# A graph network on one core: edge product of the mean pass in float32r parts, node phases in a new order, registers read earlier

## The reference, cut to what matters

```python
h = relu(layernorm(x))                                # layer norm, no weights
# L0, the mean layer: the message is made from the DESTINATION's features
msg    = relu(concat(h[dst], edge_attr_16) @ W1 + b1)
aggr   = segment_sum(msg, dst) / max(count(dst), 1)
x      = x + relu(aggr + h @ Wres + bres)
# L1: layer norm again, then three transformer convolutions (2, 2 and 1 heads)
h      = relu(layernorm(x))
for l in 0, 1, 2:
    e     = edge_attr_32 @ We
    alpha = sum(q[dst] * (k[src] + e)) / sqrt(C)      # softmax over the edges of a node
    h     = segment_sum(softmax(alpha) * (v[src] + e), dst) + h @ Ws + bs
x      = x + h                                        # PReLU between the layers
```

## Time and profile before

| what | us |
|---|---|
| median of three runs | 6319.2 |
| the profiled execution: its own time | 6324.56 |
| its span in the trace | 6322.9 |
| setup and `first` (to the mean pass's first edge product) | 0 to 71 |
| mean pass | 71 to 529 |
| `mean_end` | 529 to 611 |
| three attention passes with their node phases | 611 to 6323 |

### The profile page before, as it was taken

How to read it: one execution, slowest core, us unless ns; L and a number is a source line. 1 busy time by engine, 2 the same in 40 slices (tenths; PEclk the granted TensorE clock), 3 DMA queues, 4 the chain that set the end, 5 groups by cost and what they waited for, 6 DMA issues and landing times. The chain is left out here.

```text
span 6322.9 us, 195109 instructions
## 1 busy us (share of the span) xinstructions
PE 5496.1 (87%) x49308; PEld 4056.9 (64%) x49308; DVE 5504.6 (87%) x18553; ACT 2823.5 (45%) x12163; POOL 4385.8 (69%) x4735
## 2 busy tenths in 40 slices
PE   7996888888888887889888888888888888888887
PEld 5775666666666666666666666666666666666665
DVE  6556999999999998999999898988899899898988
ACT  3223555555555555455555555555333333333333
POOL 1223777777777775777777777775777777777775
PEclk9998999999999998999999999998899999999998
DMA  4554343333333333333333333333433333333333
GB/s 126 159 159 112 101 103 100 102 101 102 100 103 101 101 101 102 102 102 102 101 101 101 101 103 101 101 101 99 105 103 101 101 101 101 104 101 101 101 101 83
DMA packets 732940, 662.52 MB, mean 105 GB/s; under 512 B 421004, under 2 KB 558158, under 8 KB 732878
## 3 DMA queue, kind: packets, MB, share of 16 engines
q0 software_dynamic: 148544, 293.76, 18.8%
q1 hardware_dynamic: 555242, 315.06, 18.3%
q10 hardware_dynamic: 29092, 52.97, 2.7%
HBM read 639.39 MB, written 21.78 MB: 105 GB/s over the span
## 5 line engine op out<-in xcount | busy, mean ns | idle before, releaser
L1935 POOL DMA_INDIRECT Gall<-KV,sdn x4440 | 4234.5, 954 | 1377.6 <-issue 1272.7
L1220 ACT ACTIVATE vals<-vj,vals 128x32 f32<-128x32 f32 (+1 forms) x7960 | 1796.6, 313 | 19.3
L1154 PE MATMUL pG<-KVH,ohB 128*128 128x512 f32 (+1 forms) x2574 | 1176.4, 460 | 221.7 <-DVE cont L887 184.5
L1213 ACT ACTIVATE vals<-dd 128x16 f32<-128x16 f32 (+1 forms) x606 | 131.8, 217 | 2705.1 <-DVE dd L1022 2668.2
L1154 PE MATMUL pG<-KVH,ohA 128*128 128x512 f32 (+1 forms) x2574 | 1116.3, 434 | 11.8 <-DVE fw L975 0.6
L1154 PE MATMUL pG<-KVL,ohB 128*128 128x512 f32 (+1 forms) x2574 | 1072.2, 417 | 0.0
L1154 PE MATMUL pG<-KVL,ohA 128*128 128x512 f32 (+1 forms) x2574 | 1000.9, 392 | 0.0
L1147 PE MATMUL pY<-O,vals 128*66 128x42 f32 (+1 forms) x10576 | 778.9, 237 | 0.0
L1154 PEld LDWEIGHTS pG<-KVH,ohB 128*128 128x128 f32 x2574 | 530.0, 206 | 381.8 <-issue 260.9
L1147 PEld LDWEIGHTS pY<-O,vals 128*66 128x66 f32 (+1 forms) x10576 | 705.9, 143 | 46.9 <-ACT vals L1227 34.1
L1154 PEld LDWEIGHTS pG<-KVH,ohA 128*128 128x128 f32 x2574 | 494.7, 192 | 149.2 <-issue 8.6
(11 more groups left out here) (265 smaller groups left out, 8477.0 us busy)
## 6 DMA issues: line engine op xcount, KB each, us to landing
db<-D SPq DMA_DIRECT2D x606, 256.0 KB, 3.9
ea<-in_ea SPq DMA_DIRECT2D x606, 128.0 KB
Gall<-KV,sdn POOLq DMA_INDIRECT x4440
db<-D ACTq DMA_DIRECT2D x202, 256.0 KB, 3.5
qw<-QT SPq DMA_DIRECT2D x1818, 5.2 KB
dr<-in_dr SPq DMA_DIRECT2D x1212, 4.0 KB
ea<-in_ea SPq DMA_DIRECT2D x202, 64.0 KB, 3.5
sdn<-in_sdn SPq DMA_DIRECT2D x606, 12.0 KB
```

The lines of the kernel that those rows point to most:

```text
L1154: p = e.matmul(pG[:, 0:128 * m], table[:, n, :], half[:, 4 * q:4 * q + m, :].rearrange("p t c -> p (t c)"), start=n == 0 and h == 0, stop= ...
L1213: return e.activation(vals[u][:, :, 64:64 + H], dd[:, :, 0:H], ACT.Exp, scale=scale)
L1220: i = e.activation(vals[u][:, j, C * h:C * h + C], vj[u][:, j, C * h:C * h + C], ACT.Identity, scale=vals[u][:, j, 64 + h:65 + h])
L1935: e.indirect_dma_start(G[u][:, j, :], None, kvtab, bass.IndirectOffsetOnAxis(ap=sdn[u][:, j:j + 1], axis=0)).then_inc(s_g[u], 16)
```

## The change

- **Edge product.** `ea` is loaded as 64 rows: four tiles x 16 attributes, the two halves of the block side by side in the columns. ScalarE (`a_hi`) copies it as float32r into rows 0 to 63 of a new buffer `eap`, VectorE (`v_lo`) puts what is left into rows 64 to 127. The weights `bdp` are the float32r copy of W1's block diagonal (four tiles, rows 0 to 63 and again 64 to 127), and the rest of it. The product is four float32r matmuls of 256 columns. In each step ScalarE has one more operation (ahead of `relu`), VectorE one more (behind `OT`); the edge product waits for `v_lo`, and SyncE's load of `ea` waits for the `v_lo` of three blocks earlier.
- **Node phases.** Parts are now 4, 4, 3 and 2 chunks. The squares go to ScalarE (`square_A`). The norm is cut into `center`, `spread` and `scale_rows`, and folds (in `mean_end`) or the query work (in `first`) stand between them; TensorE's and ScalarE's programs take the chunks one after another with a lead of two. The norm of part 0 and the centring of part 1 of `first` (`vector_early`) stand in the middle of `vector_setup`.
- **Weights.** SyncE loads those of `first` with a semaphore of their own, which alone `first` waits for, then those of layer 0; GpSimd issues those of layers 1 and 2.
- **Registers.** In the last iteration of an attention pass the places are read ahead of the steps, also those of the drain.

```diff
+    bdp = sb("bdp", [128, 2, 256], F32R)
+    eap = nc.alloc_sbuf_tensor_at("eap", [128, 3, 256], F32R, offset=nc.sbuf_base - 256 * T)
...
-                "V": ["C acc", "Z src", "Z O", "Z OT"],
+                "V": ["C acc", "Z src", "Z O", "Z OT", "Z lo"],
                 "P": ["A e", "B agg7", "A q"],
-                "A": ["A relu"],
+                "A": ["Z hi", "A relu"],
...
+        def a_hi(e, s):
+            u = s.slot
+            ge16(e, s_e, 1, s)
+            after(e, "P", "e", s - 3)
+            return e.activation(eap[0:64, u, :], ea[u][0:64, :], ACT.Copy)
+
+        def v_lo(e, s):
+            u = s.slot
+            after(e, "A", "hi", s)
+            return e.tensor_tensor(eap[64:128, u, :], ea[u][0:64, :], eap[0:64, u, :].bitcast(F32), ALU.subtract)
...
-            return e.matmul(pE[u][:, :], ea[u][:, 0:128], bd16[:, :], start=True, stop=False)
+            after(e, "V", "lo", s)
+            hold(e)
+            for h in range(2):
+                for k in range(2):
+                    p = e.matmul(pE[u][:, 256 * h:256 * h + 256], eap[:, u, 128 * h:128 * h + 128], bdp[:, k, :],
+                                 start=h == 0 and k == 0, stop=False)
+            return p
...
             if not att and not fresh(s):
-                after(e, "P", "e", s - 3)
+                after(e, "V", "lo", s - 3)
                 hold(e)
...
+                e.dma_start(ea[u][0:64, :].rearrange("p (h c) -> p h c", h=2),
+                            eat[bass.ds(b, 1)].rearrange("a (h p) c -> p (a h) c", h=2)).then_inc(s_e[u], 16)
...
+        def vector_mean_end(e):
+            for c in chunks_of[0]:
+                fold_V_ops(e, c)
+            for n in range(NP):
+                nx = chunks_of[n + 1]
+                center(e, n)
+                for c in nx[:1]:
+                    fold_V_ops(e, c)
+                spread(e, n)
+                for c in nx[1:2]:
+                    fold_V_ops(e, c)
+                scale_rows(e, n)
+                for c in nx[2:]:
+                    fold_V_ops(e, c)
+
+        def vector_early(e):
+            e.wait_ge(s_x, 16)
+            center(e, 0)
+            center(e, 1)
+            spread(e, 0)
+            scale_rows(e, 0)
+
+        def vector_first(e):
+            for n in range(1, NP):
+                was = chunks_of[n - 1]
+                if n > 1:
+                    center(e, n)
+                    query_V(e, was[0])
+                spread(e, n)
+                query_V(e, was[1 if n > 1 else 0])
+                scale_rows(e, n)
+                for c in was[2 if n > 1 else 1:]:
+                    query_V(e, c)
+            for c in chunks_of[NP - 1]:
+                query_V(e, c)
...
+        def scalar_mean_end(e):
+            square_A(e, 0)
+            root_A(e, 0)
+            for n in range(NP):
+                cs = chunks_of[n]
+                soon = n == NP - 2
+                columns_A(e, cs[0])
+                if soon:
+                    square_A(e, n + 1)
+                for c in cs[1:2]:
+                    columns_A(e, c)
+                for k, c in enumerate(cs):
+                    rows_A(e, c)
+                    if k == 0 and soon:
+                        root_A(e, n + 1)
+                    if k == 1 and not soon and n + 1 < NP:
+                        square_A(e, n + 1)
+                    for x in cs[k + 2:k + 3]:
+                        columns_A(e, x)
+                if n + 1 < NP and not soon:
+                    root_A(e, n + 1)
...
         def vector_drain(e, n):
-            for s in (s3, s2, s1, s0):
-                base_of[s.c] = base_at(e, s)
...
-            if "D" in on:
+            if "D" in on and not last:
                 base_of[dt.c] = base_at(e, dt)
...
+                ends = [At(n, c + z.peel) for c in (-1, 0, 1, 2)]
                 for c in range(1 + z.peel, 4 + z.peel):
+                    base_of[c - 2] = base_at(e, At(whole, c - 2))
+                    for s in {2: ends[0:2], 3: ends[2:4]}.get(c - z.peel, []):
+                        drained[s.c] = base_at(e, s)
                     vector_step(e, At(whole, c), FULL, last=True)
+                base_of.update(drained)
```

More of the change, by code:

```diff
@@ L260, in sync_setup, with layer_weights @@
         e.dma_start(pra[:, :], a["prelu"].rearrange("(a m) -> a m", a=1).to_broadcast([128, 1])).then_inc(s_w, 16)
+    def layer_weights(e, l, landed):
+        for m, c in enumerate("kvqs"):
+            e.dma_start(wn[0:64, l + 1, 64 * m:64 * m + 64], a[f"W{c}{l}"]).then_inc(landed, 16)
+            e.dma_start(wn[64:65, l + 1, 64 * m:64 * m + 64], row(a[f"b{c}{l}"], 1)).then_inc(landed, 16)
+        for j in range(4):
+            e.dma_start(bd32[32 * j:32 * j + 32, l, 64 * j:64 * j + 64], a[f"We{l}"]).then_inc(landed, 16)
     def scalar_setup(e):
@@ L437, in build @@
     tiles_of = [min(4, NT - 4 * c) for c in range(NG)]
-    PART = 4
-    parts = [(c, min(c + PART, NG)) for c in range(0, NG, PART)]
+    parts = [(0, 0)]
+    while NG - parts[-1][1] > 5:
+        parts.append((parts[-1][1], parts[-1][1] + 4))
+    left = NG - parts[-1][1]
+    parts += [(NG - left, NG - left // 2), (NG - left // 2, NG)]
+    parts = [p for p in parts if p[1] > p[0]]
+    NP = len(parts)
+    part_of = [next(n for n, p in enumerate(parts) if p[0] <= c < p[1]) for c in range(NG)]
     s_kv = [sem(f"kv_landed{k}") for k in range(SL)]
@@ L460, in node_phase @@
         if norm:
-            rounds = [(range(*parts[n]) if n < len(parts) else (), range(*parts[n - 1]) if n else (),
-                       range(*parts[n - 1]) if n else ()) for n in range(len(parts) + 1)]
+            rounds = []
         elif tables:
@@ L468, in node_phase @@
         late = range(NG) if kv is not None else ()
+        chunks_of = [list(range(*p)) for p in parts] + [[], []]
         fold_V = ["den", "rcp", "avg", "val"] + {"mid": ["neg", "act"]}.get(kind, ["xr"])
         end_V = fold_V[-1]
-        norm_V = ["sum", "mean", "cen", "sq", "ssq", "var", "rstd", "nrm"]
+        center_V, spread_V, scale_V = ["sum", "mean", "cen"], ["ssq", "var"], ["rstd", "nrm"]
         col_bank = (pE[2], pY)
@@ L529, in tensor @@
                 for c in ta:
-                    if kv is not None:
-                        rows_P(e, c)
-                    else:
-                        query_P(e, c)
+                    rows_P(e, c)
+            if kind == "mean":
+                tensor_mean(e)
+            if kind == "first":
+                tensor_first(e)
             if between is not None:
@@ L586, in scalar @@
             for n, (fo, co, ta) in enumerate(rounds):
-                if norm:
-                    for c in co:
-                        columns_A(e, c)
-                    if fo:
-                        ts = slice(4 * fo[0], min(4 * fo[-1] + 4, NT))
-                        e.wait_ge(own["V"], pV["var", n])
-                        e.activation(st[:, 2, ts], st[:, 1, ts], ACT.Sqrt).then_inc(own["A"], 1)
-                if tables and not norm:
+                if tables:
                     for c in co:
@@ L597, in scalar @@
                 for c in ta:
-                    if kv is not None:
-                        rows_A(e, c)
-                    else:
-                        query_A(e, c)
+                    rows_A(e, c)
+            if kind == "mean":
+                scalar_mean_end(e)
+            if kind == "first":
+                scalar_first(e)
             for c in late:
@@ L687, in vector @@
                         fold_V_ops(e, c)
-                if norm and fo:
-                    norm_V_ops(e, n, fo)
-                if kv is None:
-                    for c in ta:
-                        query_V(e, c)
+            if kind == "mean":
+                vector_mean_end(e)
+            if kind == "first":
+                vector_first(e)
             if between is not None:
```

229 lines of the change are left out of this document (171 added, 58 removed).

## The result

The changed kernel takes 6370.9 us (median of four runs, 6361.4 to 6375.8) against 6319.4 (6319.1 to 6323.5) for the kernel before, measured on the same chip: ratio 1.0079, 95% interval 1.0067 to 1.0091. It is slower by some 51 us; 6300 was forecast. Its profiled execution took 6367.76 us, 43.2 more than that of before (6324.56). Two executions further down, one of the kernel before (14927 us) and one of `old_product` (12862), took twice as long as all others of the same kernel; the ratios leave them out, and without it the median of `old_product` would be 6307.6 instead of 6308.9.

The account below looks back on a forecast made before the run. SyncE's queue was taken to bound the mean pass at 2.24 us a block, VectorE the other stages. Edge product +2, `first` -7, `mean_end` -9, attention ends -5 sum to -19 us: median 6300.2 us, range 6288 to 6314.

Parts of the forecast that it names:

- the part on the edge product: Mean pass: shorter product hidden behind SyncE's queue, new ea load issued in 0.36 us like now; +2 us, between 0 and +8.
- TensorE's floor: Mean pass: a step's matmuls with the old product take TensorE 2.10 us, less than SyncE's 2.24.
- the second floor: Mean pass without SyncE: sums to node part, to relu, to next sums take 2.10 us, without the edge product.
- Rival 3: Mean pass: the three-dimensional load needs an extra shape instruction on SyncE, 0.129 us a block, +26 us, 6326; chance 0.07.
- Rival 1: Node phases: square not in the root's table set, 12 more loads on ScalarE, about 10 us in the path, 6310; chance 0.07.
- Rival 2: Node phases stay bound, by TensorE at half clock: -3 and -5 instead of -7 and -9, 6308; chance 0.13.
- Rival 4: Mean pass: chain of hi, lo and product longer than thought, SyncE waits; 0.1 us a block, +20 us, 6320; chance 0.04.
- Rival 6: Mean pass: TensorE's clock falls to its lower level in a tenth of the blocks, +22 us, 6322; chance 0.03.
- Both have room: Mean pass: with the added operations VectorE needs 2.03 us at most and ScalarE 1.4, within the 2.24 us step.
- Rival 5: Mean pass: SyncE is not the bound, so the pass falls to 2.10 us a block, 28 us less, 6270; chance 0.04.
- Node phases: Less VectorE work and waiting: first -7 us (-11 to -3), mean_end -9 us (-12 to -5).
- Early reads: Attention passes' ends: register reads moved to where the step begins win 5 us, between -7 and -2.

Follow-up runs that it names:

- old_product: Experiment 2: the changed kernel with the float32 edge product and plain load of before, keeping its node phases, weights and early reads; 6308.9 us, ratio 0.998.
- flat_load: The changed kernel with edge features laid out by the host as 64 plain rows of 256 numbers, so the ea load is plain; 6343.4 us.
- before_3d_load_128: The kernel before with the three-dimensional ea load from the fourth block on, its float32 product still reading 128 rows; 6373.6 us, ratio 1.0084.
- experiment 10: old_product with the ea loads issued by GpSimd instead of SyncE; 6285.9 us, ratio 0.9944.
- before_3d_load: The kernel before with the three-dimensional ea load and its float32 product reading 64 of the 128 rows; 6741.9 us.
- experiment 9: flat_load with ea loads issued by GpSimd and the edge product's first two matmuls done twice; mean pass at 2.328 us a step.

## Why the prediction was wrong

**The step that failed** is in the part on the edge product: "The new `ea` pattern has three dimensions. The nearest issue of that kind, the store of KV, takes 0.36 us, like now." It takes 0.63 us, with a register or without. The row was the wrong neighbour: the KV store has 128 rows, the new load 64, and 64 plain rows already cost 0.49 (`flat_load`); the second piece in each of them adds the other 0.14. The term was priced +2 (0 to +8); it measured +54 by itself (`before_3d_load_128`).

**The bound was right, which is why the error was dear.** That SyncE's queue sets the pass at 2.24 us and TensorE's floor is 2.10 held: 2.238 in experiment 2, and 2.10 in most stretches of experiment 10 (2.18 to 2.19 in the others, where GpSimd stood). So did the second floor, which has no edge product in it, nearly: 2.05 to 2.09 for the 2.10 worked out, and it is why a shorter product could win almost nothing even with SyncE out of the way. Whoever has shown that a queue is full has shown that each ns added to it counts 199 times; the forecast then took its one new instruction from a row on which nothing depended, and the upper bound of +8 left no room for a longer issue (0.04 us a block).

**Rival 3 had the mechanism**, a dearer three-dimensional issue with SyncE as the bound, and the point from which it decides (0.095 us a block). Its price of 0.129 us, an extra shape instruction, was wrong in kind: no such instruction came, the issue itself grew, by 0.27. It got a chance of 0.07, and the range was drawn to rivals 1 and 2 and ended at 6314, below even rival 3's own 6326.

**Rivals 4 and 6 hid behind it.** With the load cheap, the chain holds the pass at 2.2 instead of 2.10, and GpSimd's stands with the clock dips behind them add some 0.05. "Both have room" was true of each engine's sum of work and said nothing of the ring: the 1.4 us given from `ea` at X to the product took no account of the `db` issue, which stands between relu and the upper part in ScalarE's program. Rival 6's sign was right too: in the changed kernel waits at the product of 0.2 to 0.7 us, in a step that also has 0.4 us less work, went with 30 us windows down to 0.83 among those at 1.00, where the kernel before stayed at 1.00. The new product is not needed for it: `before_3d_load_128`, with the old one but waits for late data of up to 2 us, was at 0.97 too. The Trainium skill (TensorE: Matmul & The Clock Gate, A second HAM failure mode: psum-queue depth-cycling), cited for this rival, agrees with the trace so far as short idles went with a swinging clock.

**Rival 5** asked for 6270 if SyncE was not the bound; SyncE was the bound.

**Node phases**: -4.9 and -6.7 for -7 and -9, inside both ranges. VectorE's last operation of `first` ended at 64.4 us, not 62: 3.4 us of it is a wait for the last part's queries on ScalarE, which itself waited for TensorE's product. Rival 1 is out: no further table load, three as before. Rival 2, TensorE's products as the bound of the node phases, holds in part by that wait; no run separates its share.

**Early reads**: nothing for -5. The forecast named the covers ("three of them under the wait for the last gathers") without a row that shows a wait at that place; there was none.

By its own list the forecast was to be called wrong if the pass changed by more than 8 us, and a pace above 2.3 was to mean rival 3 or 4: both came. It said a rival 3 or 4 would show in "a new instruction in SyncE's queue"; it showed in an old one's duration.

The Trainium skill (Perfetto Trace Analysis, What "DMA-bound" means) names as one kind of DMA-bound kernel the one whose issuing sequencer's track is solid with DMA slices. Here SyncE's holds 0.99 us of them in 2.51, and is the bound all the same: the rest is register reads and arithmetic, which the busy tables leave out (one table read takes 0.64 us here).

## What to carry to other kernels

When a queue of one engine sets the pace of a loop, look up each instruction that a change puts in it by its own shape (rows, pieces, row length), and if no row has that shape, take the dearest of its kind as the bound, times the loop's count. Before reshaping a load so that another engine works less, ask whether an idle engine can issue it; here that one move was worth 60 us to the changed kernel and 23 to the old product. When an operation enters a ring of engines, follow the ring through each program's order, waits and issues included; adding up each engine's work does not find it.

## What was not expected of the hardware

- Time to issue one `ea` load on SyncE's queue: 128 rows of 512 bytes 0.362 us; 64 rows of 2 x 512 bytes 0.626 (fixed address 0.611); 64 rows of 1 KB 0.488; 64 rows of 512 bytes (32 KB) 0.480; 128 rows of 1 KB (128 KB) 0.362. With 64 rows in one piece each the bytes make no difference (0.480, 0.488), and half as many rows cost a third more than 128. Why stays open; the number of pieces alone does not set it, since 128 pieces in 64 rows cost 0.26 us more than 128 pieces in 128.
- GpSimd issues the same loads in 0.526 us (64 plain rows) and 0.602 (three-dimensional), and 128 plain rows of 512 bytes in 0.544: there 64 rows are not dearer than 128. The Trainium skill (DMA: Bandwidth & Descriptors, Anatomy of one DMA — SWDGE (gpsimd) path) calls the making of descriptors there small, with many to be had before it shows; the trace agrees, twice the pieces being 0.076 us. On SyncE's queue, which set the pace, the same step is 0.138 (0.488 to 0.626).
- TensorE, with its float32 product reading 64 rows (`before_3d_load`) instead of 128 (`before_3d_load_128`) and all else the same but for the form of the first three loads, stayed at the granted clock of 0.50 for the whole pass though it was busy all the time: 4.34 us a block instead of 2.50, in all four executions (6739.8 to 6742.3 us).
- GpSimd, when it issues two loads a block, stands still for 2.8 to 4.2 us after every 108 or 123 issues (experiment 9).
